# One perceiver block on one core: the state-space part spread over three batches, and the expansion to channels done by four 32-row products

## The chip, the cores and the metric

The kernel runs on one NeuronCore of a Trainium2 chip. The metric is the device time of one execution in microseconds; the time before is the median of three runs, 1502.03 us (1501.18 to 1503.05). All numbers below are microseconds unless they say otherwise.

## The reference, cut to what matters

128 sequences of 32 queries with 256 channels attend to 257 context rows each (16 heads of 16 channels), then pass a state-space layer and a mixture of experts:

```
x = x + cross_attention(layernorm(x), ctx, mask)      # (128, 32, 256), context (128, 257, 256)
x = x + state_space(layernorm(x))
x = x + experts(layernorm(x))                         # 8 experts, the best 2 of each token
```

Two details of it matter here. The softmax is divided out late: the kernel multiplies unnormalised probabilities with the values, and then multiplies each channel of the result with the reciprocal of its head's sum. And the state-space layer is `out = Y[0] / norm`:

```
proj = xs @ W_in.T                   # C, B and x of 256 columns each, and dt
conv_out = sum_k xp[:, k:k+s] * conv_w[:, k] + conv_b
A = A_param * softplus(dt + bias)
Y = ssd(xh, A, Bh, Ch)               # Y_diag = einsum(C, B, exp(segsum(A)), x)
norm = exp(cumA) * cumsum(exp(-cumA))
```

Only `Y[0]`, the result of the first sequence, is used, so `ssd` is computed once for 32 positions, and the norm for every sequence.

## The kernel before, in words

The first phase (`attend`, lines 115 to 1385) goes over 32 tiles of 128 tokens; a tile has four batches (sequences) b = 0 to 3 of 32 queries. The second (`experts`) goes over 71 tiles of tokens sorted by expert. The change is in the first alone.

Each engine has its own program, written out by hand as a function `tile(i)` with a loop over b; the engines meet in semaphores, and the order within an engine is the order of its `tile`. Tiles 0 to 3 and the last ones are unrolled, the rest is a hardware loop. The work is staggered: while TensorE weighs the values of batch n, it transposes the probabilities of n+1 and projects keys and values (k and v, 24 products in a split precision) of n+2. In each batch TensorE does `turn_c`, `project_k`, `project_v`, `turn_a`, `weigh_values`, `transpose_probs(.., 0)`, `turn_b`, `transpose_probs(.., 1)`, `scores`. `turn_a`, `turn_b` and `turn_c` hold the small products of the tiles before: expansion, attention's output, dt, the sums of the decay, the router.

PSUM has eight banks: K (keys, later the weighed values OT and the sums RP), V_ (values, and the second half of the transposed probabilities), four banks SC for the scores, PT, and M, which all the small products share one after the other. The names that the prediction follows:

- `px` (lines 1320 to 1330, GpSimd): per query the reciprocal of each head's sum, and the last context row's probability times it, laid out by group of heads, 128 queries and heads by 32 columns. `mm(RP, px, sel)` (line 492) is the last product of `weigh_values` and releases `o_ready`. ScalarE copies RP to `rp` (`take_rp`).
- `o_ready` also releases ScalarE's copy of the next values (`take_values`, line 724). The second `transpose_probs` writes the bank V_ and so waits for that copy (`v_done`, line 472).
- `expand` (line 512): four products with constant matrices `er` and `ep` bring the 32 rows of `rp` to 256 channels, twice (reciprocals and last probabilities), in M. VectorE's `weigh` (line 926) multiplies them with the weighed values and the last values; `attention_out` adds them.
- `ssd` (lines 572, 783 and 1136 for TensorE, ScalarE and VectorE): runs once, in batch 0 of tile 2, ahead of the second transposes. It projects the first sequence (24 instructions), VectorE convolves in a chain of linked instructions, TensorE forms C times B per head, then the segment sums, ScalarE takes the exponential, VectorE multiplies and masks 16 times into `w4` (each head's weights four times side by side), and 16 products with x fill all 128 rows of M, which ScalarE copies to `y0`. All of it is one chain over one bank; the other engines' tile work stands meanwhile.

Of the kernel before, what the change touches and what calls it, by code (L numbers as in the profile page):

```python
# [4 lines left out]
F32 = mybir.dt.float32  # L5
# [109 lines left out]
def attend(nc, xd, ctxd, ctxl, maskd, pard, wxbcd, cond, padd, wgd, wud, wdd, d_high, d_low, zbuf, table, outd, con, cst, wg, wu, wd,  # L115
# [7 lines left out]
    with own:  # L123
# [53 lines left out]
        px = sb("px", [P, 2, 2, NH, NG, 2])  # L177
# [42 lines left out]
        w4 = carve(H * P)[0:Q].rearrange("p (h b l) -> p h b l", h=H, b=TB)  # L220
# [4 lines left out]
        SC = [ps(f"sc{r}") for r in range(NG)]  # L225
# [3 lines left out]
        RP = K[0:2 * H, NH * 2 * Q:NH * 2 * Q + Q]  # L229
# [41 lines left out]
        NSOFT = len(ATANH) + 6  # L271
        PLAN = 10
# [30 lines left out]
        def _(sp):  # L303
# [77 lines left out]
            sp.wait_ge(ssd_act, 4)  # L381
# [28 lines left out]
        def _(pe):  # L410
# [161 lines left out]
            def ssd():  # L572

                pe.wait_ge(wxbc_in, 16)
                pe.wait_ge(a_done, 1)
                pe.wait_ge(norm_done, 1)
# [5 lines left out]
                pe.wait_ge(ssd_dve, 11)  # L582
# [4 lines left out]
                pe.wait_ge(ssd_act, 1)  # L587
                pe.wait_ge(ssd_dve, 12)
                mm(M[0:Q, :], cst("gt")[0:Q, :], at_[:, :, :].rearrange("p h l -> p (h l)")).then_inc(ssd_pe, 1)
                pe.wait_ge(ssd_act, 2)  # L590
# [4 lines left out]
                pe.wait_ge(ssd_dve, 14)  # L595
                for h in range(H):
                    last = mm(M[:, h * HD:(h + 1) * HD], w4[:, h, :, :].rearrange("p b l -> p (b l)"),
                              xs[:, h * HD:(h + 1) * HD])
                last.then_inc(ssd_pe, 1)
                pe.wait_ge(ssd_act, 4)  # L600


            def turn_a(i, b):
                if b == 0 and runs(i - 1):
                    if runs(i - 2):
                        pe.wait_ge(en_done, i - 1)
                    if isinstance(i, int) and i == 1:
                        pe.wait_ge(z1T_done, 3)
                    expand(i - 1)
# [13 lines left out]
            def turn_b(i, b):  # L623
                if b == 0 and (runs(i - 2) or runs(i - 3)):
                    if runs(i - 1):
                        pe.wait_ge(t_done, 2 * i)
                    sum_decay_and_rank(i - 2, i - 3)
                    if isinstance(i, int) and i == 2:
                        ssd()
# [15 lines left out]
            def turn_c(i, b):  # L645
                if b == 0 and runs(i - 1):
                    if runs(i - 2):
                        pe.wait_ge(norm_done, i - 1)
                    if runs(i - 3):
                        pe.wait_ge(chosen_done, i - 1)  # L650
                    project_out(i - 1)
# [4 lines left out]
                if b == 2 and runs(i - 2):  # L656
                    if runs(i - 1):
                        pe.wait_ge(dt_done, i)
                    turn_z3(i - 2)
                if b == 3 and runs(i - 1):  # L660
# [4 lines left out]
                    sum_a(i - 1)  # L665

# [19 lines left out]
            pe.wait_ge(blank_rows, 1)  # L686
# [25 lines left out]
        def _(act):  # L712
# [35 lines left out]
            def take_rp(i, b):  # L748
                n = 4 * i + b
                act.wait_ge(ou_done, n + 1)  # L750
                act.wait_ge(blank_rows, 1)
                if b == 0:
                    at_least(act, ex_ready, i)
                copy(rp[0:2 * H, b * Q:(b + 1) * Q], RP).then_inc(rp_done, 1)
# [28 lines left out]
            def ssd():  # L783
                act.wait_ge(ssd_pe, 2)
                copy(gs[:, :, :].rearrange("p h l -> p (h l)"), M[0:Q, :]).then_inc(ssd_act, 1)
                act.wait_ge(ssd_pe, 3)
                nc.scalar.activation(ls[:, :, :].rearrange("p h l -> p (h l)"), M[0:Q, :], ACT.Exp).then_inc(ssd_act, 1)
# [19 lines left out]
            def tile(i, k=None):  # L807
                for b in range(TB):
# [7 lines left out]
                    if b == 0 and runs(i - 2):  # L816
                        decays(i - 2)
                    if b == 2 and runs(i - 1):
# [7 lines left out]
                    if b == 0 and isinstance(i, int) and i == 2:  # L826
                        ssd()
# [8 lines left out]
                    if b == 3 and runs(i + 2):  # L836
                        take_z1T(i + 2)
                    if b != 0 and runs(i):
# [25 lines left out]
        def _(dve):  # L864
# [61 lines left out]
            def weigh(j):  # L926
# [3 lines left out]
                EX = M[:, :].rearrange("p (k a n) -> p k a n", k=2, a=NH)  # L930
# [205 lines left out]
            def ssd():  # L1136
                k = [0]

                def link(ins):
                    k[0] += 1  # L1140
                    ins.then_inc(ssd_dve, 1)
                    dve.wait_ge(ssd_dve, k[0])


                dve.wait_ge(ssd_pe, 1)
                link(V.memset(xp[:, :, 0:KC - 1], 0.0))
                link(V.tensor_copy(xp[:, :, KC - 1:], M[:, 0:NC * Q].rearrange("p (c l) -> p c l", c=NC)))
# [5 lines left out]
                link(V.tensor_tensor(cv[:, 0], xp[:, :, 0:Q], tap(0), ALU.mult))  # L1153
                for n in range(1, KC):
                    link(V.tensor_tensor(cv[:, 1], xp[:, :, n:n + Q], tap(n), ALU.mult))
                    link(V.tensor_tensor(cv[:, 0], cv[:, 0], cv[:, 1], ALU.add))
                link(V.tensor_tensor(cT, cv[:, 0], prm("convb").unsqueeze(2).broadcast_to([P, NC, Q]), ALU.add))
# [4 lines left out]
                link(last)  # L1162
                le = cst("le")[0:Q, :].unsqueeze(1).broadcast_to([Q, H, Q])
                link(V.tensor_tensor(at_, dtv[0:Q, 5, :].unsqueeze(2).broadcast_to([Q, H, Q]), le, ALU.mult))
                dve.wait_ge(ssd_act, 2)
                link(V.tensor_tensor(ws, gs, ls, ALU.mult))
                for h in range(H):
                    last = V.tensor_tensor(w4[:, h], ws[:, h, :].unsqueeze(1).broadcast_to([Q, TB, Q]),
                                           cst("le")[0:Q, :].unsqueeze(1).broadcast_to([Q, TB, Q]), ALU.mult)
                link(last)  # L1170
                assert k[0] == 14, k[0]
                dve.wait_ge(ssd_act, 4)

            def tile(i):
                for b in range(TB):
# [35 lines left out]
                    if b == 0 and runs(i + 2):  # L1211
                        statistics1(i + 2)
                    if b == 0 and runs(i - 1):
                        weigh(i - 1)
                        attention_out(i - 1)
                    if b == 1 and runs(i - 1):
# [27 lines left out]
                    if b == 0 and isinstance(i, int) and i == 2:  # L1244
                        ssd()
# [4 lines left out]
                    if b == 2 and runs(i - 1):  # L1250
                        soft_in(i - 1)

            V.memset(chosen[:, :], 0.0).then_inc(chosen_done, 1)
            V.memset(rp[:, :], 0.0).then_inc(blank_rows, 1)
# [3 lines left out]
            V.tensor_copy(tokf[:, :], cst("tok")).then_inc(init, 1)  # L1258
            dve.wait_ge(init, 2)
# [21 lines left out]
        def _(pool):  # L1281
# [38 lines left out]
            def last_probs(i, b):  # L1320
# [5 lines left out]
                for k in range(2):  # L1326
                    G.tensor_tensor(px[:, b % 2, k].rearrange("p a g h -> p g a h"),
# [53 lines left out]
            split_low(0, 2)  # L1381
            last_probs(0, 0)
# [384 lines left out]
```

## Time and profile before

| | |
|---|---|
| median of three runs | 1502.03 |
| the profiled execution | 1488.71 |
| its span | 1486.7 |
| TensorE busy | 1410.8 (95%) |
| VectorE busy | 1124.9 (76%) |
| ScalarE busy | 996.1 (67%) |
| GpSimd busy | 833.8 (56%) |
| share of TensorE in the chain that ended last | 84% |

The trace has each instruction's start and length. A matmul in fp32 runs as two instructions, and in a row of the timeline equal instructions that follow each other are merged (x8). Matmuls are pipelined: each takes some 0.2 to 0.4 from start to end, while the next starts 0.1 after it, so it is starts that tell what TensorE spends; the ends tell when others can go on. The busy share is an average over a loop in which TensorE is gapless, one tile with the state-space part, and the experts.

### The profile page before, as it was taken

What the parts mean: (1) busy time and instruction counts of PE and PEld (TensorE: products, weight loads), DVE (VectorE), ACT (ScalarE), POOL (GpSimd) and SP (SyncE); (2) the same over time, 40 slices, a digit from 0 to 9 for tenths busy, and PEclk for the clock granted to TensorE, in tenths of its full rate; (3) what the DMA queues carried; (4) which work ended last, traced back from release to release, by engine and by line L of the source; (5) the groups of instructions that cost most, each with busy time, mean ns of one, the idle gap of its engine ahead of it and who ended that gap; (6) DMA issues with size and microseconds to landing.
All of it is one profiled execution on the core that took longest, in us unless ns stands there. A gap on an engine that the chain in (4) does not pass through costs nothing.

```text
span 1486.7 us, 53570 instructions
## 1 busy us (share of the span) xinstructions
PE 1410.8 (95%) x15668; PEld 1288.0 (87%) x15669; DVE 1124.9 (76%) x3999; ACT 996.1 (67%) x2482; POOL 833.8 (56%) x1401
## 2 busy tenths in 40 slices
PE   6969999999999999999999998579999999999997
PEld 5858888888888888888888887379999999999997
DVE  3647888888888888888888886468878777787775
ACT  4726777777777777777777775067777776777674
POOL 3514665665666656656656553236666665565554
PEclk9969999999999999999999998589999999999999
DMA  6212464454433433433433321435655555555554
GB/s 189 67 30 73 120 200 136 144 192 131 122 98 96 127 93 99 122 101 90 126 96 106 86 70 55 159 120 149 162 141 151 158 142 145 144 163 142 141 147 111
DMA packets 102009, 183.80 MB, mean 124 GB/s; under 512 B 19393, under 2 KB 61377, under 8 KB 101793
## 3 DMA queue, kind: packets, MB, share of 16 engines
q1 hardware_dynamic: 86272, 164.35, 36.5%
q0 software_dynamic: 15680, 18.76, 7.1%
q8 instruction: 28, 0.46, 0.1%
q14 instruction: 29, 0.23, 0.1%
HBM read 152.63 MB, written 31.13 MB: 124 GB/s over the span
## 4 chain that ended last, share of the span: by engine, by line
PE 84%; DMA 2%; issue 2%; POOL 2%; DVE 1%; ACT 1%; POOLq 1%; DVEq 0%; ACTq 0%; SPq 0%
PE k L412 16%; PE m L412 12%; PE v_p L412 11%; PE y_p L1478 9%; PE up_p L1478 9%; PE gate_p L1478 8%; PE sc L412 5%; PE pt L476 5%; PE v_p L476 4%; PE ht_p L1517 3%; PE m L496 2%; DMA par<-zbuf,gi 2%; PE z_p L1484 1%; POOL gi L1668 1%; POOLq L1667 0%
## 5 line engine op out<-in xcount | busy, mean ns | idle before, releaser
L738 ACT ACTIVATE wd<-wd,nmx 128x257 f32<-128x257 f32 x512 | 255.7, 503 | 31.0 <-DVE nmx L884 26.7
L714 ACT ACTIVATE wd<-v_p 128x512 f32<-128x512 f32 x256 | 152.6, 596 | 163.8 <-PE k L412 136.5
L1305 POOL TENSOR_TENSOR ctx_lo<-wd,ctx_hi 128x516 fp32r<-128x516 f32 x128 | 167.0, 1304 | 130.5 <-ACT ctx_hi L714 130.5
L884 DVE CUSTOM_DVE_ANT_0 wd<-sc,wd 128x257 f32<-128x257 f32 x512 | 191.4, 421 | 63.6 <-PE sc L412 57.3
L1680 POOL DMA_INDIRECT out<-par,oi x71 | 113.5, 1599 | 146.5 <-ACT par L1586 145.9
L412 PE MATMUL k<-ctx_hi,wkh 128*128 128x256 f32 x512 | 159.3, 311 | 1.7 <-POOL ctx_lo L1305 1.4
L1557 ACT ACTIVATE uw_hi<-wu 128x1408 fp32r x71 | 98.3, 1385 | 85.1 <-PE up_p L1478 84.8
L1668 POOL COPY oi<-par 128x4 int32 x71 | 148.1, 2087 | 0.0
L1615 DVE TENSOR_TENSOR uw_lo<-wu,uw_hi 128x1408 fp32r<-128x1408 f32 x71 | 115.4, 1625 | 41.3 <-ACT uw_hi L1557 41.3
L412 PE MATMUL k<-ctx_lo,wkh 128*128 128x256 f32 x512 | 145.3, 284 | 0.0
L1615 DVE TENSOR_TENSOR gw_lo<-wg,gw_hi 128x1408 fp32r<-128x1408 f32 x71 | 115.4, 1625 | 39.2 <-ACT gw_hi L1557 39.2
L412 PE MATMUL k<-ctx_hi,wkl 128*128 128x256 f32 x512 | 145.0, 283 | 0.0
L412 PE MATMUL v_p<-wvh,ctx_lo 128*128 128x256 f32 x512 | 143.7, 281 | 0.0
L412 PE MATMUL v_p<-wvh,ctx_hi 128*128 128x256 f32 x512 | 143.4, 280 | 0.0
L412 PE MATMUL v_p<-wvl,ctx_hi 128*128 128x256 f32 x512 | 142.6, 279 | 0.0
L873 DVE TENSOR_SCALAR kT<-k,par 128x256 f32<-128x256 f32 x256 | 114.1, 477 | 24.3 <-PE k L412 23.6
L1668 POOL COPY gi<-par 128x4 int32 x71 | 122.2, 1721 | 10.3 <-issue 5.7
L1478 PE MATMUL y_p<-wd,hT_hi 128*128 x426 | 121.1, 284 | 1.9 <-DVE hT_lo L1615 1.9
L1478 PE MATMUL y_p<-wd,hT_lo 128*128 x426 | 120.5, 283 | 0.0
L1478 PE MATMUL y_p<-dl,hT_hi 128*128 128x256 f32 x426 | 120.1, 282 | 0.0
L1557 ACT ACTIVATE gw_hi<-wg 128x1408 fp32r x71 | 98.1, 1382 | 13.9 <-PEq L123 8.7
L1674 POOL DMA_INDIRECT par<-zbuf,gi x71 | 73.2, 1031 | 60.3 <-POOL gi L1668 53.3
(200 smaller groups left out, 4678.8 us busy)
## 6 DMA issues: line engine op xcount, KB each, us to landing
dl<-d_low SPq DMA_DIRECT2D x71, 768.0 KB, 4.4
wd<-in_ctx SPq DMA_DIRECT2D x128, 258.0 KB, 2.7
wd<-in_mask SPq DMA_DIRECT2D x512, 32.1 KB, 1.8
wd<-in_wd SPq DMA_DIRECT2D x24, 256.0 KB
d_high<-wd SPq DMA_DIRECT2D x24, 256.0 KB
d_low<-wd SPq DMA_DIRECT2D x24, 256.0 KB
wd<-d_high SPq DMA_DIRECT2D x8, 768.0 KB, 9.2
wg<-in_wg SPq DMA_DIRECT2D x8, 704.0 KB
```

The lines of the kernel that those rows point to most:

```text
L412: return nc.tensor.matmul(out, lhsT, rhs, start=start, stop=stop)
L476: last = nc.tensor.transpose((PT, V_)[d][:, o:o + P], pr[:, g, t * P:(t + 1) * P], ident)
L714: return nc.scalar.activation(out, in_, ACT.Copy, **kw)
L738: nc.scalar.activation(pr[:, g, :], sm[:, g, :], ACT.Exp, bias=nmx[:, g:g + 1], scale=-1.0, accum_out=rsum[:, g:g + 1]).then_inc(exp_done, 1)
L873: V.tensor_scalar(kT[:, b % 2, a, 0:LAST], K2[:, a, :], prm("bk")[:, a:a + 1], None, ALU.add).then_inc(k_done, 1)
L884: V.tensor_tensor_reduce(sm[:, g, :], SC[g][:, 0:S], msk[:, b, :], -1.0, 3.0e38, ALU.add, ALU.min, nmx[:, g:g + 1]).then_inc(max_done, 1)
L1305: G.tensor_tensor(ctx_lo[:, b % 2], ctx[:, b], ctx_hi[:, b % 2].bitcast(F32), ALU.subtract).then_inc(lo_done, 1)
L1478: return nc.tensor.matmul(out, lhsT, rhs, start=start, stop=stop)
L1557: nc.scalar.activation(dst, src, ACT.Copy).then_inc(done, 1)
L1615: V.tensor_tensor(dst, src, hi.bitcast(F32), ALU.subtract).then_inc(done, 1)
L1668: G.tensor_copy(dst.unsqueeze(1), tab[:, bass.ds(col, 1), :]).then_inc(done, 1)
L1680: G.indirect_dma_start(outd[:, :], bass.IndirectOffsetOnAxis(oi[:, s, 1:2].bitcast(U32), 0), yb[:, s, :], None, compute_op=ALU.add).then_i ...
```

## The change

- `expand` uses one constant `spread` (128x128) and four row groups: rows 32r to 32r+31 of `rp` against the same rows of `spread`, each into its own score bank. For that the four kinds of sums must stand on different row groups: `px` gets 128 columns, 32 per kind with 8 in use (the rest set to zero once), RP and `rp` have all 128 rows.
- As the expansion now writes score banks, it waits for the maxima of the batch before them, and the scores of batch 2 wait for `weigh`. It no longer waits for M's users (`en_done`), and the sums in `turn_b` no longer wait for `weigh`.
- VectorE does `weigh` and `attention_out` before the statistics of a later tile.
- `ssd` is cut into pieces: the projection ahead of batch 3 of tile 1, the convolution on VectorE at that batch's end, the segment sums ahead of batch 0 of tile 2 in the bank PT, the rest (`ssd_mix`) where all of it was. The mask is multiplied in once, on C times B; the 16 masked copies fall away, and the last products are 64 of 32x32 instead of 16 of 32x128.

```
 def expand(j):
     pe.wait_ge(rp_done, 4 * (j + 1))
-    for k, e in enumerate(("er", "ep")):
-        for a in range(NH):
-            o = (k * NH + a) * P
-            last = mm(M[:, o:o + P], cst(e)[:, a * P:(a + 1) * P], rp[:, :])
+    if runs(j + 1):
+        pe.wait_ge(max_done, 4 * (4 * (j + 1) + 2))
+    for r in range(NG):
+        rows = slice(r * Q, (r + 1) * Q)
+        last = mm(SC[r][:, 0:P], spread[rows, :], rp[rows, :])
     last.then_inc(ex_ready, 1)
...
-        px = sb("px", [P, 2, 2, NH, NG, 2])
+        px = sb("px", [P, 2, 2 * NH, Q])
+        spread = sb("spread", [P, P])
...
-        RP = K[0:2 * H, NH * 2 * Q:NH * 2 * Q + Q]
+        RP = K[:, NH * 2 * Q:NH * 2 * Q + Q]
...
-    mm(RP, px[:, b % 2].rearrange("p k a g h -> p (k a g h)"), cst("sel")).then_inc(o_ready, 1)
+    mm(RP, px[:, b % 2].rearrange("p k n -> p (k n)"), cst("sel")).then_inc(o_ready, 1)
...
 def scores(i, b):
+    if b == 2 and runs(i - 1):
+        pe.wait_ge(t_done, 2 * i)
...
+def ssd_project():
+    pe.wait_ge(wxbc_in, 16)
+    pe.wait_ge(dt_done, 1)
...
+def ssd_sums(n):
+    pe.wait_ge(pt_done, 2 * n - 1)
+    pe.wait_ge(ssd_dve, SSD_A)
+    mm(PT[0:Q, :], cst("gt")[0:Q, :], at_[:, :, :].rearrange("p h l -> p (h l)")).then_inc(ssd_pe, 1)
+
+def ssd_mix():
+    pe.wait_ge(norm_done, 1)
+    pe.wait_ge(ssd_dve, SSD_C)
...
+    pe.wait_ge(ssd_act, 2)
+    pe.wait_ge(ssd_dve, SSD_C + 2)
+    for h in range(H):
+        for b in range(TB):
+            last = mm(M[b * Q:(b + 1) * Q, h * HD:(h + 1) * HD], ws[:, h, :], xs[:, h * HD:(h + 1) * HD])
...
 # VectorE
-    for h in range(H):
-        last = V.tensor_tensor(w4[:, h], ws[:, h, :].unsqueeze(1).broadcast_to([Q, TB, Q]),
-                               cst("le")[0:Q, :].unsqueeze(1).broadcast_to([Q, TB, Q]), ALU.mult)
+    ssd_step(V.tensor_tensor(gs, M[0:Q, :].rearrange("p (h l) -> p h l", h=H), le, ALU.mult))
+    ssd_step(V.tensor_tensor(ws, gs, ls, ALU.mult))
...
 # TensorE: where the pieces go
+    if b == 2 and isinstance(i, int) and i == 1:      # turn_c
+        ssd_project()
...
-        pe.wait_ge(dt_done, i)                        # turn_b, b == 3: turn_z1 in tile 1
+        pe.wait_ge(ssd_dve, SSD_X)
...
     sum_a(i - 1)                                      # turn_c, b == 3
+    if isinstance(i, int) and i == 1:
+        ssd_sums(TB * (i + 1) + 1)
```

## Rows read from the trace of the kernel before

**Rows 1.** Busy time by stage: us, busy (xcount) of each engine, clock, DMA, GB/s.
```profile
138.08:904.99 766.91, 765.53 (x10528) 673.50 (x10527) 630.28 (x3079) 556.28 (x1733) 465.04 (x973) 1.00 0.40 116
81.33:138.08 56.75, 45.31 (x439) 37.39 (x437) 29.53 (x126) 20.92 (x65) 13.47 (x32) 0.73 0.15 38
86.00:116.70 30.70, 20.14 (x88) 14.91 (x88) 11.05 (x40) 6.18 (x17) 1.29 (x1) 0.50 0.02 4
```

**Rows 2.** Timeline of TensorE, steady tile: start, length, engine, line, operation, count.
```profile
247.64 0.28 PE L412 MATMUL v_p<-wvh,ctx_lo 128*128 128x256 f32 x1
247.75 1.05 PE L412 MATMUL m<-rp,con 128*128 128x128 f32 x8
248.74 0.65 PE L412 MATMUL k<-wd 128*32 128x64 f32 x32
249.21 0.23 PE L412 MATMUL k<-con,px 128*32 128x32 f32 x2
249.36 0.66 PE L476 MATMUL pt<-con,wd 128*128 128x128 f32 x4
...
250.22 0.37 PE L412 MATMUL m<-chosen,con 128*128 128x8 f32 x2
250.44 0.63 PE L476 MATMUL v_p<-con,wd 128*128 128x128 f32 x4
251.01 0.69 PE L412 MATMUL sc<-kT,qbd 32*64 32x257 f32 x16
251.63 1.13 PE L412 MATMUL m<-par,aT 128*128 128x256 f32 x4
```

**Rows 3.** Timeline of TensorE, tile 1 (values product to weighing).
```profile
61.98 0.28 PE L412 MATMUL v_p<-wvh,ctx_lo 128*128 128x256 f32 x1
62.19 0.65 PE L412 MATMUL k<-wd 128*32 128x64 f32 x32
```

**Rows 4.** Timeline of TensorE, steady tile, behind the scores.
```profile
271.94 0.40 PE L412 MATMUL m<-dtv,con 128*128 128x16 f32 x2
```

**Rows 5.** Timeline of TensorE, third and fourth batch of the steady tile.
```profile
264.48 0.63 PE L476 MATMUL v_p<-con,wd 128*128 128x128 f32 x4
...
269.70 0.22 PE L412 MATMUL k<-con,px 128*32 128x32 f32 x2
...
270.35 0.38 PE L496 MATMUL m<-con,wd 128*128 128x128 f32 x2
270.77 0.63 PE L476 MATMUL v_p<-con,wd 128*128 128x128 f32 x4
```

**Rows 6.** Timeline of ScalarE, the same two batches.
```profile
263.80 0.60 ACT L714 ACTIVATE wd<-v_p 128x512 f32<-128x512 f32 x1 [1.20 <-PE k L412]
...
270.03 0.60 ACT L714 ACTIVATE wd<-v_p 128x512 f32<-128x512 f32 x1 [1.16 <-PE k L412]
```

**Rows 7.** Timeline of TensorE in the state-space part.
```profile
84.57 3.98 PE L412 MATMUL m<-z2T,wg 128*128 128x32 f32 x24 [0.84 <-DVE dtv L1012]
93.09 1.92 PE L412 MATMUL m<-wg 128*32 128x256 f32 x4 [4.54 <-DVE wg L1160]
95.68 1.91 PE L412 MATMUL m<-wg,con 32*32 32x512 f32 x2 [0.68 <-ACT wg L714]
...
102.49 6.97 PE L412 MATMUL m<-wg 32*128 32x16 f32 x32 [3.61 <-DVE wg L1168]
110.52 1.08 PE L476 MATMUL v_p<-con,wd 128*128 128x128 f32 x4 [1.05 <-ACT wd L714]
```

**Rows 8.** Timeline of VectorE ahead of and in the state-space part.
```profile
77.23 0.16 DVE L1007 TENSOR_TENSOR dtv<-sc,par 128x16 f32<-128x16 f32 x1
...
88.73 0.36 DVE L1147 COPY wg<-m 128x192 f32<-128x192 f32 x1
...
98.32 0.68 DVE L1166 TENSOR_TENSOR wg<-wg 32x512 f32<-32x512 f32 x1 [4.57 <-ACT wg L787]
```

**Rows 9.** Chain of waits, the end of attention: start, length, what.
```profile
926.86 2.09 PE m L412 x8
```

More of the change, by code:

```diff
@@ L224, in attend @@
         K2 = K[:, 0:NH * LAST].rearrange("p (a t) -> p a t", a=NH)
-        SC = [ps(f"sc{r}") for r in range(NG)]
+        SCORES = own.enter_context(nc.psum_tensor("sc", [P, NG, 512], F32))
+        SC = [SCORES[:, r, :] for r in range(NG)]
         PT = ps("pt")
@@ L271, in attend @@
         NSOFT = len(ATANH) + 6
+        SSD_X, SSD_A, SSD_C = 2, 3, 12
         PLAN = 10
@@ L593, in ssd @@
                 last.then_inc(ssd_pe, 1)
-                pe.wait_ge(ssd_act, 3)
-                pe.wait_ge(ssd_dve, 14)
-                for h in range(H):
[L597 to L600, printed above, removed]
+                pe.wait_ge(ssd_act, 2)
[3 more added lines that the diff above has]
+                        last = mm(M[b * Q:(b + 1) * Q, h * HD:(h + 1) * HD], ws[:, h, :], xs[:, h * HD:(h + 1) * HD])
+                last.then_inc(ssd_pe, 1)
+                pe.wait_ge(ssd_act, 3)
             def turn_a(i, b):
                 if b == 0 and runs(i - 1):
[L605 to L608, printed above, removed]
                     expand(i - 1)
@@ L624, in turn_b @@
                 if b == 0 and (runs(i - 2) or runs(i - 3)):
-                    if runs(i - 1):
-                        pe.wait_ge(t_done, 2 * i)
                     sum_decay_and_rank(i - 2, i - 3)
                     if isinstance(i, int) and i == 2:
-                        ssd()
+                        ssd_mix()
                 if b == 1 and runs(i - 2):
@@ L665, in turn_c @@
                     sum_a(i - 1)
+                    if isinstance(i, int) and i == 1:
+                        ssd_sums(TB * (i + 1) + 1)
             def tile(i):
@@ L750, in take_rp @@
                 act.wait_ge(ou_done, n + 1)
-                act.wait_ge(blank_rows, 1)
                 if b == 0:
                     at_least(act, ex_ready, i)
-                copy(rp[0:2 * H, b * Q:(b + 1) * Q], RP).then_inc(rp_done, 1)
+                copy(rp[:, b * Q:(b + 1) * Q], RP).then_inc(rp_done, 1)
             def take2(dst, ready, done, j):
@@ L781, in gate_exp, with ssd_exp, ssd_out @@
                 nc.scalar.activation(sv[:, 1, 0:1], sv[:, 0, 0:1], ACT.Exp).then_inc(gate_e, 1)
-            def ssd():
+            def ssd_exp():
                 act.wait_ge(ssd_pe, 2)
-                copy(gs[:, :, :].rearrange("p h l -> p (h l)"), M[0:Q, :]).then_inc(ssd_act, 1)
-                act.wait_ge(ssd_pe, 3)
-                nc.scalar.activation(ls[:, :, :].rearrange("p h l -> p (h l)"), M[0:Q, :], ACT.Exp).then_inc(ssd_act, 1)
+                nc.scalar.activation(ls[:, :, :].rearrange("p h l -> p (h l)"), PT[0:Q, :], ACT.Exp).then_inc(ssd_act, 1)
+            def ssd_out():
                 act.wait_ge(ssd_pe, 4)
@@ L817, in tile @@
                         decays(i - 2)
+                    if b == 0 and isinstance(i, int) and i == 2:
+                        ssd_exp()
                     if b == 2 and runs(i - 1):
@@ L837, in tile @@
                         take_z1T(i + 2)
+                    if b == 0 and isinstance(i, int) and i == 2:
+                        ssd_out()
                     if b != 0 and runs(i):
@@ L1134, in plan_tiles, with ssd_step, ssd_conv @@
                               ).then_inc(info_done, 1)
[L1136 to L1142, printed above, removed]
-                dve.wait_ge(ssd_pe, 1)
-                link(V.memset(xp[:, :, 0:KC - 1], 0.0))
-                link(V.tensor_copy(xp[:, :, KC - 1:], M[:, 0:NC * Q].rearrange("p (c l) -> p c l", c=NC)))
+            ssd_steps = [0]
+            def ssd_step(ins):
+                ssd_steps[0] += 1
+                ins.then_inc(ssd_dve, 1)
+                dve.wait_ge(ssd_dve, ssd_steps[0])
+            def ssd_conv():
+                le = cst("le")[0:Q, :].unsqueeze(1).broadcast_to([Q, H, Q])
+                dve.wait_ge(ssd_pe, 1)
+                ssd_step(V.memset(xp[:, :, 0:KC - 1], 0.0))
+                ssd_step(V.tensor_copy(xp[:, :, KC - 1:], M[:, 0:NC * Q].rearrange("p (c l) -> p c l", c=NC)))
+                assert ssd_steps[0] == SSD_X
+                dve.wait_ge(a_done, 1)
+                ssd_step(V.tensor_tensor(at_, dtv[0:Q, 5, :].unsqueeze(2).broadcast_to([Q, H, Q]), le, ALU.mult))
+                assert ssd_steps[0] == SSD_A
                 taps = prm("convw").rearrange("p (c k) -> p c k", k=KC)
@@ L1161, in ssd, with ssd_weights @@
                                            cst("bm8").unsqueeze(2).broadcast_to([P, n8, Q]), ALU.mult)
-                link(last)
+                ssd_step(last)
+                assert ssd_steps[0] == SSD_C
+            def ssd_weights():
                 le = cst("le")[0:Q, :].unsqueeze(1).broadcast_to([Q, H, Q])
[L1164 to L1167, printed above, removed]
-                    last = V.tensor_tensor(w4[:, h], ws[:, h, :].unsqueeze(1).broadcast_to([Q, TB, Q]),
-                                           cst("le")[0:Q, :].unsqueeze(1).broadcast_to([Q, TB, Q]), ALU.mult)
-                link(last)
-                assert k[0] == 14, k[0]
-                dve.wait_ge(ssd_act, 4)
+                dve.wait_ge(ssd_pe, 3)
+                ssd_step(V.tensor_tensor(gs, M[0:Q, :].rearrange("p (h l) -> p h l", h=H), le, ALU.mult))
+                dve.wait_ge(ssd_act, 1)
+                ssd_step(V.tensor_tensor(ws, gs, ls, ALU.mult))
+                dve.wait_ge(ssd_act, 3)
             def tile(i):
@@ L1215, in tile @@
                         attention_out(i - 1)
+                    if b == 0 and runs(i + 2):
+                        statistics1(i + 2)
                     if b == 1 and runs(i - 1):
@@ L1251, in tile @@
                         soft_in(i - 1)
+                    if b == 3 and isinstance(i, int) and i == 1:
+                        ssd_conv()
             V.memset(chosen[:, :], 0.0).then_inc(chosen_done, 1)
-            V.memset(rp[:, :], 0.0).then_inc(blank_rows, 1)
+            V.memset(px[:, :, :, :].rearrange("p b k n -> p (b k n)"), 0.0).then_inc(blank_rows, 1)
             V.memset(pay[:, :, :].rearrange("p k c -> p (k c)"), 0).then_inc(init, 1)
@@ L1258, in _ @@
             V.tensor_copy(tokf[:, :], cst("tok")).then_inc(init, 1)
+            V.tensor_copy(spread[:, :].rearrange("p (h d) -> p h d", d=HD),
+                          cst("sel")[:, 0:P // HD].unsqueeze(2).broadcast_to([P, P // HD, HD])).then_inc(blank_rows, 1)
             dve.wait_ge(init, 2)
```

34 lines of the change are left out of this document (12 added, 22 removed).

## The prediction

> **What bounds the kernel now.** I read the stages first, then the order of time on TensorE, then the other engines at the places that looked tight. In the attention loop 28 tiles take 766.91 us, 27.39 each, and TensorE is busy for 765.53 of them at the full clock [rows 1]: every ns that TensorE issues more or less per tile counts. The one tile in which the state-space part (SSD) runs takes 56.75, so 29.36 more, much of it at a granted clock of 0.50 [rows 1]. The expert phase is not touched. The change acts on three things: the expansion (once a tile), the product with px (once a batch, four a tile), and the SSD part (once).
>
> **The expansion.** Today four products, two instructions each, take from 247.75 to 248.74; from the last values product to the next stage it is 1.10 (247.64 to 248.74) [rows 2]. Where no expansion stands between, the same step takes 0.21 (61.98 to 62.19) [rows 3]. So it costs 0.89. One 128-column instruction takes (1.05 - 0.28)/7 = 0.11. The 0.21 is such a stream plus 0.10, which every change of the array's shape shows. The new form has four products on 32 rows each, in four banks. The nearest row is the scores: 32x64 pieces, eight side by side, two rounds of 257 columns, 0.62 from 251.01 to 251.63 [rows 2]. Two streams of 257 columns are 0.43, so 0.19 is first load, issue and changeover. With 128 columns the streams are 0.22; the load is twice as wide (+0.05) and there are fewer pieces (-0.02): 0.44. The values product now also hands over to another shape (0.21 for 0.11): 0.65 instead of 1.10, **-0.45 a tile**. Bounds: if the wide loads of the row groups came one after another, eight times 0.11 plus a last stream and changeover, 1.28, **+0.18**; if nothing but the two streams counted, -0.6.
>
> **The product with px.** It keeps its 32 columns of result but its weights grow from 32 to 128 columns, so it leaves the 32-column shape of the products before it, and has the full shape. Today the pair starts at 249.21 and the transposes at 249.36: 0.15, of which 0.10 is the changeover, so about 0.04 for the pair [rows 2]. The same kind of pair with full weights and few columns, chosen, takes 0.22 (250.22 to 250.44) although it streams 8 columns: its loads set the pace, 0.11 each [rows 2]. So TensorE pays 0.22 - 0.04 = +0.18 a batch (bounds: 0.02, if the loads hid behind the products before; 0.23, if the transposes' first load were pushed out too).
> What waits for the pair is worse off. The pair dtv, the first behind a changeover, takes 0.40 from start to end [rows 4]; px today 0.22 to 0.23. With the changeover now ahead of it (it starts 0.11 later), its end comes **0.29 later**. ScalarE's copy of the values waits for that, and the second transposes wait for the copy. In the third batch the copy ends at 263.80 + 0.60 = 264.40 and the transposes start at 264.48; in the fourth 270.63 and 270.77, while TensorE's own work ran out at about 270.57 (270.35 and two instructions of 0.11) [rows 5, 6]. These two batches have no slack and pay 0.29 each. The first two have longer products ahead of those transposes (in the first dtv, lg and chosen [rows 2]) and pay 0.18. Per tile 2 x 0.18 + 2 x 0.29 = **+0.94**. That ScalarE now copies 128 rows of RP in place of 32 costs nothing, as its time goes by columns (rp copies are off the path).
> One rule of the Trainium skill bears on this. The rows show 0.11 for a full-width load, 0.03 from one px instruction to the other. The page "TensorE: Matmul & The Clock Gate", section "LDWEIGHTS (loading the stationary operand)", says that a load's time goes by its columns, at columns/1.2 ns, however many rows it has: an estimate by it is 107 for 27 ns, +0.16 a batch, 20 us over 128 batches, and with it alone the sum below would end 8 us lower, as it has no waiting copy in it.
>
> **Waits that move.** The wait for weigh's two products goes from ahead of the decay sums to ahead of the scores; no row of the steady tile shows an idle time there [rows 2]. The expansion now waits for the four maxima of the next batch, which VectorE has behind it by its own order, and VectorE does weigh before the statistics. All at nothing, hidden under TensorE's 24 k and v products. Without that cover each would cost an instruction or two of VectorE's, 0.36 to 0.68 [rows 8], a tile.
> Per tile: -0.45 + 0.94 = **+0.49**; 28 tiles: +13.7. Tiles 1, 2 and 31 have stalls that take part of it: +1.0 together. Steady sum **+14.7**.
>
> **The SSD part.** Before, in its tile [rows 7, 8]: a wait of 0.84 and the projection (84.57, 24 instructions at half clock), VectorE's convolution from 88.73 (TensorE idle 4.54), products at 93.09, sums at 95.68, transposes, the masking of 16 weights (TensorE idle 3.61), 32 instructions from 102.49, copies, until 110.52; then 6.2 us at half clock until 116.70. New:
> - projection in the tile before: 24 loads of 0.11 = 2.7 on TensorE's path, at full clock;
> - z1's transposes wait until VectorE has copied the projection. VectorE gets there behind the second head and a (77.23 + 0.16), then needs 0.45 for memset and copy and semaphore time: 1.3 that TensorE waits;
> - the sums as a product of their own: 1.91 at half clock [rows 7], so 1.0;
> - the convolution (the 4.54 for which TensorE idles today [rows 7], less the 0.6 that come before the sums: 3.9) delays VectorE's maxima and keys; the 24 k and v products, 0.12 each, hide 2.9 of it, the rest comes back before the expansion and weigh: 0.8;
> - the wait for norms, with VectorE late: 1.7 in place of 0.84;
> - the mix: four products 0.9, masking at the 0.68 of the same shape [rows 8] and handover 0.9, the second multiply or transposes and copy of x 1.0, 128 small instructions at the k<-wd pace (0.47 for 32 [rows 2]) 1.9, handover and copy of y 0.5: 5.2. Of the 16 maskings nothing is left.
> Sum 12.7. TensorE streams little in these stretches, and today the clock falls after just such a stretch and costs 3.1 behind it. I take 3.9 for that: 16.6 against 29.36, **-12.7**. Bounds: full clock throughout -16.9; clock down already from the projection on, the work between doubled, -8.
> In the tail, at half clock, the last expansion (2.09 [rows 9]) is on the chain: -1.2, px there +0.5: **-0.7**.
>
> **Sum**: 14.7 - 12.7 - 0.7 = +1.3. The profiled execution took 1488.71 (span 1486.7), which becomes 1490.0; the runs' median is 1502.03, of which none of these stages is known to hold the other 13, so I carry the difference over: **1503.3**.
>
> **Rivals.**
> - Clock falls early. For it: the clock is 0.50 from 86.00 on, though TensorE was busy there, with loads more than streams; the projection now brings 2.7 us of that a tile earlier. Against: it is followed by dense k and v products. Saves 8 only: 1508.
> - Full clock throughout: the waits are now short and split. Against: the mix still has 5 us of handovers. Saves 16.9: 1499.
> - Wide px loads are hidden (0.02 a batch): then a tile changes by -0.37, so 11 less instead of 15 more, with the rest 1478; with part of it hidden, around 1490. For it: 32-column loads hide today. Against: the chosen and dtv pairs don't.
> - The row groups' loads come one after another: it decides once the eight loads cost 0.3 more than the streams hide (9 us in 30 tiles); in full +0.18 in place of -0.45, 30 tiles, +19: 1522, slower. Against: the scores' sixteen loads fit into 0.62.
> - The change doesn't do what it says on the maskings or products: excluded by the diff, no time of its own.
>
> **Chances.** Forecast (gain and loss cancel) 0.43; clock early 0.17; full clock 0.15; px loads hidden in whole or part 0.16; loads serial 0.09. Range of the forecast itself 1498 to 1508; with the clock's cases and partly hidden px loads 1489 to 1513, which leaves out the ends of the last two. About 0.2% (3 us) is what a measurement of this kernel can tell from no change. Faster: 0.15 of the px case, 0.09 of full clock, 0.09 of the forecast's own spread = 0.33. Slower: 0.09 serial, 0.14 clock early, 0.12 of the forecast = 0.35. Same: 0.32.
>
> **What would show it.** The distance between two expansions in the loop: 27.88 for 27.39. From the values product to weigh's products: 0.65. From the px pair's first to the transposes: 0.22 or more, and the second transposes of the last two batches 0.29 later than now. The tile with the SSD mix near 39, the one before it 5 to 6 longer than it was. It is wrong if the tile distance falls (px loads hidden), or exceeds 28.2 (loads serial), or if SSD's two tiles together give back less than 8 or more than 17.

## The result, and the profile after

| | before | changed |
|---|---|---|
| median of 7 and 7 runs on one chip | 1502.72 (1501.18 to 1503.64) | 1506.13 (1505.37 to 1509.19) |
| ratio, 95% interval | | 1.0028 [1.0016, 1.004] |
| the profiled execution (span) | 1488.71 (1486.7) | 1506.13 (1504.1) |
| attention loop, 28 tiles [rows 1] | 766.91 | 798.01 |
| the tile with the SSD mix [rows 1] | 56.75 | 39.20 |
| TensorE at half clock, one stretch [rows 1] | 30.70 | 13.65 |
| TensorE busy | 1410.8 | 1415.3 |

The kernel became 3.4 us slower, and 1506.13 lies within the forecast's range (1503.3, 1489 to 1513). The profiled execution of before, 1488.71, lies outside that chip's own timed runs of the same kernel (1501.18 to 1503.64), so the two profiles can't be subtracted as a whole. Below they are compared tile by tile.

By stage, the windows of the changed kernel: the loop, the SSD tile, the half-clock stretch (columns as in [rows 1]).
```profile
129.67:927.68 798.01, 776.94 (x10528) 673.90 (x10527) 629.69 (x3078) 559.52 (x1731) 465.73 (x973) 1.00 0.39 111
90.47:129.67 39.20, 34.86 (x506) 28.29 (x506) 23.54 (x102) 21.62 (x70) 13.58 (x33) 0.83 0.22 57
93.88:107.53 13.65, 10.79 (x170) 7.38 (x171) 5.01 (x18) 4.04 (x13) 1.27 (x1) 0.50 0.08 22
```
The loop is 31.1 us longer (28.50 a tile against 27.39), while TensorE's busy time in it grew by 11.4 only, from 765.53 to 776.94. So a good part of the loss is TensorE standing still, where before [rows 1] it was gapless. The SSD tile is 17.6 shorter.

TensorE in the steady tile, from the expansion on; it answers to [rows 2].
```profile
271.61 0.50 PE L414 MATMUL sc<-rp,spread 32*128 32x128 f32 x8
272.04 0.65 PE L414 MATMUL k<-wd 128*32 128x64 f32 x32
272.63 0.41 PE L414 MATMUL k<-con,px 128*128 128x32 f32 x2
272.87 0.63 PE L480 MATMUL pt<-con,wd 128*128 128x128 f32 x4
...
274.49 0.69 PE L414 MATMUL sc<-kT,qbd 32*64 32x257 f32 x16
275.86 1.10 PE L414 MATMUL m<-par,aT 128*128 128x256 f32 x4 [0.68 <-DVE dtv L1022]
```
From the expansion to weigh's products it is now 0.43, where it was 0.99; px starts 0.24 ahead of the transposes instead of 0.15. Those are the forecast's terms. Then comes what it does not have: from the scores to attention's output 1.37 instead of 0.62, with 0.68 of idling behind the norms (line 1022). The list of waits gives it for the whole kernel:
```profile
PE m L414 <- DVE dtv L1022: 18.2, 25, 2.1
```
Its longest, 2.1, is in the SSD part; the other 24 are the loop's, 16 us together. In the same list of before the norms stand with 1.5 in 2 waits, none of them the loop's.

VectorE in before, where the statistics (line 911, as 913 behind it) are done while the expansion runs, and the norms' multiply is line 1012:
```profile
248.25 0.43 DVE L911 BATCH_NORM_STATS2 st<-wd 128x6 f32<-128x256 f32 x1
...
248.87 0.42 DVE L931 TENSOR_TENSOR t<-m,ou 128x256 f32<-128x256 f32 x1
...
250.71 0.16 DVE L1012 TENSOR_TENSOR dtv<-m,dtv 128x16 f32<-128x16 f32 x1
```
VectorE in the tile of the changed kernel shows what the wait is made of.
```profile
269.50 0.43 DVE L894 CUSTOM_DVE_ANT_0 wd<-sc,wd 128x257 f32<-128x257 f32 x1 [1.54 <-PE sc L414]
...
272.57 0.42 DVE L941 TENSOR_TENSOR t<-sc,ou 128x256 f32<-128x256 f32 x1
272.91 0.41 DVE L942 TENSOR_TENSOR t<-sc,vl 128x256 f32<-128x256 f32 x1
273.36 0.80 DVE L952 SCALAR_TENSOR_TENSOR aT<-t,par 128x128 f32<-128x128 f32 x2
274.08 0.41 DVE L921 BATCH_NORM_STATS2 st<-wd 128x6 f32<-128x256 f32 x1
274.59 0.18 DVE L923 BATCH_NORM_AGGREGATE mv<-st 128x2 f32<-128x6 f32 x1
...
275.21 0.16 DVE L1022 TENSOR_TENSOR dtv<-m,dtv 128x16 f32<-128x16 f32 x1
```
The maxima at 269.50 begin after 1.54 of idling for the scores of the fourth batch; then come the other maxima and the keys, one wait of 0.70 for ScalarE, and work without a pause up to the norms at 275.21, the statistics (274.08, 274.59) among it. The scores that it waited for, on TensorE, and GpSimd at that time:
```profile
267.72 0.69 PE L414 MATMUL sc<-kT,qbd 32*64 32x257 f32 x16
```
```profile
267.88 0.96 POOL L1358 DMA_INDIRECT slot_table<-pay,ri  x1 [0.30 <-issue]
```
The scores' last product ends at 267.72 + 0.69 = 268.41. VectorE begins 1.09 later. The release comes late in this way in all 28 tiles of the loop in this trace, by 0.9 against the traces below, each time with GpSimd's second indirect DMA (0.96 long) in progress when the scores end. In the trace of before [rows 1] no release of the scores is late, nor is one in its second trace, below, though that DMA is in progress there too at the end of the fourth batch's scores.

TensorE in the SSD part; it answers to [rows 7].
```profile
74.59 2.87 PE L414 MATMUL m<-z2T,wg 128*128 128x32 f32 x24
...
82.91 0.44 PE L500 MATMUL m<-con,wd 128*128 128x128 f32 x2 [1.14 <-DVE wg L1159]
...
84.66 1.04 PE L414 MATMUL pt<-wg,con 32*32 32x512 f32 x2
...
90.47 0.50 PE L414 MATMUL sc<-rp,spread 32*128 32x128 f32 x8 [1.70 <-DVE nmx L894]
91.26 0.65 PE L414 MATMUL k<-wd 128*32 128x64 f32 x32 [0.29 <-DVE kT L883]
...
95.00 1.91 PE L414 MATMUL m<-wg 128*32 128x256 f32 x4 [2.14 <-DVE dtv L1022]
97.68 0.61 PE L601 MATMUL m<-con,wg 128*32 128x128 f32 x2 [0.77 <-DVE wg L1184]
...
101.17 1.11 PE L480 MATMUL v_p<-con,wd 128*128 128x128 f32 x4 [0.50 <-ACT y L723]
```

### The profile page after: what moved, and what is told of

It reads as the page before. It is cut to its first block and busy times, and to the rows that moved or that the text cites. A ratio compares the mean times of both kernels' runs of the same rounds, so it can differ in the third digit from the quotient of the medians.

```text
span 1504.1 us, 53622 instructions
## 1 busy us (share of the span) xinstructions
PE 1415.3 (94%) x15764; PEld 1280.6 (85%) x15765; DVE 1124.3 (75%) x3985; ACT 999.4 (66%) x2481; POOL 834.5 (55%) x1401
## 5 line engine op out<-in xcount | busy, mean ns | idle before, releaser
L1342 POOL TENSOR_TENSOR rr<-wd,rr 128x4 f32<-128x4 f32 x128 | 25.5, 199 | 186.6 <-DVE rr L901 180.6
```

## The experiments

Before ran on three more chips, at 1486.35 (9 runs), 1483.95 (15) and 1484.17 (17), 16 to 19 us faster than on the chip of the first comparison. Ratios below are against before on the same chip. "A tile" is the median distance between two expansions in the loop; before's is 27.38 in both of its traces.

**SSD alone.** The changed kernel with `expand`, px, RP, the order of `weigh` and its waits as before.
```
-                for r in range(NG):
-                    rows = slice(r * Q, (r + 1) * Q)
-                    last = mm(SC[r][:, 0:P], spread[rows, :], rp[rows, :])
+                for k, e in enumerate(("er", "ep")):
+                    for a in range(NH):
+                        ...
+                        last = mm(M[:, o:o + P], cst(e)[:, a * P:(a + 1) * P], rp[:, :])
```


> The kernel before with the state-space part alone spread as in the change (expansion, px and VectorE's order as before). Theory (gain of the state-space part is real, what ate it is in the loop): the two tiles together 10 to 11 us shorter than before (tile 1 near 33.5, tile 2 near 39), the loop unchanged at 27.39 in the profile, so 1492 against 1502.7. Rival (the spreading itself brought little, the change's loop is innocent): within 3 us of before.

Measured: 1473.83, ratio 0.9918 [0.9905, 0.9932], so -12.5. Windows of the loop and of the tile with the mix:
```profile
126.01:893.79 767.78, 766.16 (x10528) 673.69 (x10527) 630.60 (x3078) 555.83 (x1731) 465.49 (x973) 1.00 0.40 116
89.55:126.01 36.46, 32.81 (x507) 27.29 (x508) 23.68 (x105) 21.98 (x70) 13.51 (x32) 0.91 0.24 61
```
The loop is that of before (767.78 against 766.91). The gain lies in tiles 1 and 2, which take 33.89 + 36.46 = 70.35 for 26.74 + 56.75 = 83.49: -13.1. The forecast had -12.7; the 10 to 11 expected of this run was too little; it is what these tiles give in the changed kernel (10.6).

**Wide px alone.** Before, with px and RP of 128 columns and rows, the 32 rows that count first, the expansion as it was.
```
-        px = sb("px", [P, 2, 2, NH, NG, 2])
+        px = sb("px", [P, 2, P])
-        RP = K[0:2 * H, NH * 2 * Q:NH * 2 * Q + Q]
+        RP = K[:, NH * 2 * Q:NH * 2 * Q + Q]
```


> The kernel before with px, RP and rp made 128 wide and nothing else; the expansion is the old one. Theory (two exposed full-width loads behind a changeover, and a release 0.29 later in the last two batches): tile 27.39 + 0.94 = 28.33, 28 us slower, 1530. Rival (the width costs TensorE nothing, the loss of the changed kernel is all waits for VectorE): tile 27.4, same time.

Measured: 1512.26, ratio 1.0175 [1.0161, 1.0189], +25.9. Its loop:
```profile
139.43:932.41 792.98, 788.48 (x10528) 690.31 (x10527) 636.07 (x3079) 556.88 (x1733) 464.75 (x973) 1.00 0.38 112
```
28.31 a tile, +0.93, where the forecast's term is +0.94. The first two batches take 0.18 and 0.19 more, the last two 0.28 and 0.29.

**The changed kernel with px as four column products.** Four pairs, each with 32 columns of px, each into its own 32 rows of RP.
```
-                mm(RP, px[:, b % 2].rearrange("p k n -> p (k n)"), cst("sel")).then_inc(o_ready, 1)
+                for r in range(NG):
+                    last = mm(RP[r * Q:(r + 1) * Q], px[:, b % 2, r, :], cst("sel"))
+                last.then_inc(o_ready, 1)
```


> The changed kernel with the px product as four products of 32 columns, each into its own column group, so that the shape stays that of the products before it. Theory: px costs about 0.06 to 0.1 a batch in place of 0.22, the last two batches win 0.25 or more each; in the first batch the win is swallowed by the wait for the norms, which grows by as much. Tile 28.57 - 0.75 = 27.8, 20 us faster than the changed kernel, 1486. Rival (px is hidden, the norm wait sets the tile): no more than 3 us.

Measured: 1475.47, ratio 0.992 [0.9906, 0.9934], so -10.9. TensorE around px:
```profile
266.84 0.65 PE L414 MATMUL k<-wd 128*32 128x64 f32 x32
267.31 0.24 PE L414 MATMUL k<-con,px 128*32 128x32 f32 x8
267.48 0.66 PE L480 MATMUL pt<-con,wd 128*128 128x128 f32 x4
```
The pair becomes eight instructions, and still px starts 0.17 ahead of the transposes (0.15 in before, 0.24 in the changed kernel). The px product keeps the 128x32 shape of its neighbours, so no changeover is ahead of it. Against the changed kernel's 784.2 on the other chips (below) the loop gives 16.9 back:
```profile
129.15:896.47 767.32, 757.04 (x11200) 660.41 (x11199) 629.66 (x3078) 552.60 (x1731) 464.10 (x974) 1.00 0.40 116
```
That is 27.41 a tile, 0.60 less than the changed kernel's 28.01; 0.75 was expected, counted from the trace with the late releases. The busy time is 757.04, so 10.3 are still idle. Attention's output again waits 0.30 in each tile:
```profile
270.12 1.10 PE L414 MATMUL m<-par,aT 128*128 128x256 f32 x4 [0.30 <-issue]
```
As TensorE comes to it still earlier, the norms' wait has grown: from the scores to attention's output it is 0.99, 0.37 more than in before, where the changed kernel has 0.18 more.

**Slot writes a batch earlier.** The changed kernel with the indirect DMAs of `write_slots` in batch 2 instead of 3.
```
-                    if b == 3 and runs(i - 3):
+                    if b == 2 and runs(i - 3):
                         write_slots(i - 3)
```


> The changed kernel with GpSimd's two slot writes (indirect DMAs) of a tile issued at the end of batch 2 instead of batch 3. In the changed kernel the release of the scores issued in batch 3 reaches VectorE 0.95 late in 27 tiles, while the second slot write runs, and project_out then waits 0.75 for the norms. Theory A (the slot write holds that release up): the delay leaves this place, tile near 27.85, 19 us faster, 1487. Theory B (VectorE's new order and TensorE's earlier arrival make the wait, the late release is an accident of the record): tile stays within 0.1 of 28.57 and the time within 3 us.

Measured: 1492.69, ratio 1.0042 [1.0029, 1.0056], 28.01 a tile against 28.58 in the first trace of the changed kernel. It looks like a gain of 0.57 a tile, but the chip was another. So the changed kernel itself had to be measured away from the first chip.

**The changed kernel again**, not altered.

> The changed kernel itself, so that it stands beside the others on one chip. The chip of the experiments runs the kernel before in 1486, the chip of the first comparison in 1503. Theory A (the late release of the scores in 27 tiles is a trait of that other chip and stretched the kernel before there too): here no late release, tile 28.05, 8 us slower than before. Theory B (the late release belongs to the change): tile 28.57, 22 us slower.

Measured: 1493.09, ratio 1.0058 [1.0045, 1.0072], 28.01 a tile, the loop 784.42. No release is late in this trace. The slot writes had gained nothing.

**The third chip: before again, the changed kernel a third time, the slot writes again.**

> The kernel before once more, for its own profile on the chip of the experiments. Theory (the chips differ by 16 us outside the attention loop's instructions or by late releases): on a chip near 1485 the tile is 27.39 and no release is late; on a chip near 1503 either the tile is longer, with scores released late, or the experts take longer.

> The changed kernel once more. On a chip near 1485: tile 28.01, 9 slower than before. On a chip near 1503: late releases as in its first profile, tile 28.57, 3 to 4 slower than before.

> The slot writes in batch 2 once more. On the first chip of the experiments it was level with the changed kernel on the second (tile 28.01 both), so where no release is late the place of the slot writes is worth nothing. On a chip near 1503, theory A (the slot writes hold the release up): faster than after_third by up to 15, theory B: the same.

Measured: before 1484.43, ratio 0.9996 [0.9982, 1.001]; changed 1492.87, 1.006 [1.004, 1.0079]; slot writes earlier 1493.17, 1.006 [1.0041, 1.008]. Loops of before and of the changed kernel there:
```profile
137.79:904.66 766.87, 765.53 (x10528) 673.53 (x10527) 630.41 (x3079) 556.26 (x1733) 465.18 (x973) 1.00 0.39 116
```
```profile
130.65:914.89 784.24, 776.90 (x10527) 673.87 (x10526) 628.95 (x3078) 555.21 (x1731) 464.62 (x974) 1.00 0.38 113
```
784.24 - 766.87 = 17.4, or 0.62 a tile. Here the scores of the fourth batch end at 266.87 + 0.69 = 267.56, and VectorE begins 0.20 later instead of 1.09:
```profile
266.87 0.69 PE L414 MATMUL sc<-kT,qbd 32*64 32x257 f32 x16
```
```profile
267.76 0.43 DVE L894 CUSTOM_DVE_ANT_0 wd<-sc,wd 128x257 f32<-128x257 f32 x1 [0.65 <-PE sc L414]
```
GpSimd's indirect DMA is in progress here as well when these scores end:
```profile
267.04 0.96 POOL L1358 DMA_INDIRECT slot_table<-pay,ri  x1 [0.31 <-issue]
```
This is so in 28 tiles of this trace, of after_again's and of both of before's, and none of these releases is late. So the DMA's being there does not delay the release by itself; what differs in the first trace is not shown.

Behind the expansion, VectorE's first product of `weigh` and its multiply of the norms:
```profile
271.33 0.42 DVE L941 TENSOR_TENSOR t<-sc,ou 128x256 f32<-128x256 f32 x1 [0.42 <-PE sc L414]
...
273.79 0.16 DVE L1022 TENSOR_TENSOR dtv<-m,dtv 128x16 f32<-128x16 f32 x1
```
Attention's output starts at 274.44, 3.68 behind the expansion:
```profile
270.76 0.50 PE L414 MATMUL sc<-rp,spread 32*128 32x128 f32 x8
...
274.44 1.10 PE L414 MATMUL m<-par,aT 128*128 128x256 f32 x4
```
It still waits: from the scores to it are 0.79, against 0.62 in before. The loop's norm waits have left the list of waits, in which only the 2.1 of the SSD part stands:
```profile
PE m L414 <- DVE dtv L1022: 2.1, 1, 2.1
```
So the place of the slot writes is without effect where no release is late. Whether it would change the late releases on the first chip was not shown, since no experiment ran there.

**Statistics later.** VectorE's statistics of a later tile (0.6 in all, lines 921 and 923) behind the norms instead of ahead of them.
```
                     if b == 0 and runs(i - 1):
                         weigh(i - 1)
                         attention_out(i - 1)
-                    if b == 0 and runs(i + 2):
-                        statistics1(i + 2)
...
                     if b == 0 and runs(i - 2):
                         scale_y(i - 2)
+                    if b == 0 and runs(i + 2):
+                        statistics1(i + 2)
```


> The changed kernel with VectorE's statistics of a later tile moved to the end of batch 0, behind the norms. Theory (project_out waits for the norms, because VectorE has weigh, attention_out and the statistics between the reciprocals and the norms while TensorE now comes 0.28 earlier): the wait of 0.18 a tile goes, tile 27.88, 5 us faster than the changed kernel. Rival (the wait hangs on o_ready and the heads, not on VectorE's order): tile unchanged within 0.03.

Measured: 1486.11, ratio 1.0014 [1.0005, 1.0023], 7.0 less than the changed kernel on the same chip (1493.09), and still 2.2 more than before. A tile is 27.87, the number that the forecast had for it (27.88), and from the scores to attention's output it is 0.62 again:
```profile
127.77:908.22 780.45, 776.03 (x10527) 674.19 (x10526) 633.86 (x3078) 554.91 (x1731) 464.38 (x974) 1.00 0.39 114
```
The loop gives 4.0 of the 7.0. Most of the rest lies ahead of tile 2, where the two traces differ by 2.3 (91.52 and 89.21 at its expansion), and this is not shown to be the edit's: there two traces of one program, after_third and slots_b2_again (whose edit acts from tile 3 on), differ by 2.5 on one chip.

**Both: four column products and statistics later.**

The two edits above together.

> Both mends: px as four products of 32 columns in their own column groups, and the statistics behind the norms. px_cols alone had a tile of 27.41 with 0.37 of it a wait for the norms. Theory: that wait goes, tile 27.04, 10 us faster than px_cols and 21 faster than before, 1465. Rival (another release is next, such as the copy of the values in the last two batches or weigh ahead of the scores): tile 27.3 or more, at most 4 us faster than px_cols.

Measured: 1463.56, ratio 0.9859 [0.9844, 0.9874], 20.4 faster than before and the best of all; a tile is 27.05.
```profile
128.36:886.09 757.73, 755.42 (x11200) 660.05 (x11199) 630.21 (x3078) 552.58 (x1731) 464.51 (x974) 1.00 0.40 117
```
TensorE is busy 755.42 of 757.73, all but gapless again.

**The expansion alone**, with four column products and late statistics, the SSD part as in before. Of the SSD's edits it has none, such as:
```
-    if b == 2 and isinstance(i, int) and i == 1:
-        ssd_project()
...
+    for h in range(H):
+        last = V.tensor_tensor(w4[:, h], ws[:, h, :].unsqueeze(1).broadcast_to([Q, TB, Q]),
```

> The kernel before with the expansion of the change and both mends (px as four products of 32 columns, the statistics behind the norms), the state-space part as it was. Theory (the two parts of the change add up, each acts on its own stretch): tile 27.05, 9 to 10 us faster than before, 1474 on a chip where before takes 1484; together with the 12.5 of the state-space part this gives the 20 to 22 of cols_stats_late. Rival (the parts share a gain): more than 13 or less than 6.

Measured: 1475.79, ratio 0.9935 [0.9919, 0.9952], -8.4; a tile is 27.07.
```profile
136.30:894.31 758.01, 755.85 (x11200) 660.45 (x11199) 628.45 (x3078) 553.04 (x1731) 465.46 (x974) 1.00 0.40 117
```
With SSD alone (-12.5) that makes -20.9, and both together measured -20.4: in the medians the two halves add up within their intervals (some 2 us each). The traces do not show it stage by stage: tiles 1 and 2 fall from 81.68 here to 73.48 in cols_stats_late, by 8.2, where SSD alone had 13.1, and 3.7 of the rest stand in the stretch behind the last expansion, mostly the experts, on which no edit acts.

## Why the prediction was right, and where it was right by luck

**The loop's terms** held to a few hundredths. From the last values product to weigh's it is 0.64 (0.21 + 0.43) for 1.10, the -0.45 of the expansion; the serial-loads rival (+0.18) and "two streams only" are out. px costs +0.93 a tile: 0.18 and 0.19 on TensorE in the first two batches, 0.28 and 0.29 in the last two, where the values' copy releases the transposes. The fourth batch of the changed kernel, TensorE and then ScalarE; it answers to [rows 5, 6]:
```profile
265.91 0.41 PE L414 MATMUL k<-con,px 128*128 128x32 f32 x2
266.16 0.64 PE L480 MATMUL pt<-con,wd 128*128 128x128 f32 x4
266.63 0.38 PE L500 MATMUL m<-con,wd 128*128 128x128 f32 x2
267.16 0.63 PE L480 MATMUL v_p<-con,wd 128*128 128x128 f32 x4
```
```profile
266.42 0.60 ACT L723 ACTIVATE wd<-v_p 128x512 f32<-128x512 f32 x1 [1.46 <-PE k L414]
```
The copy ends at 266.42 + 0.60 = 267.02, the transposes start at 267.16, and TensorE's own work ran out at 266.63 + 0.22 = 266.85, as the forecast's chain has it. The rivals with hidden px loads are out. Column products show what hidden costs: 0.02 in each of the first two batches. The Trainium skill's page "TensorE: Matmul & The Clock Gate", "Part 3: Packing small matmuls — row/col tiling", says that products in different column groups run concurrently in the array; the trace agrees with it: from the first of the four column products to the transposes (eight instructions) it is 0.17, where one 32-column pair had 0.15 and the wide pair 0.24.

**The step that failed** is "Waits that move", all of which the forecast put "at nothing". It looked for idle time in the rows of before and found none at attention's output, but did not work out how much slack was there. The change uses it up from both sides. TensorE comes to attention's output sooner: 3.88 behind the expansion in before (247.75 to 251.63), 3.50 without a wait, as stats_late shows: 0.38 sooner. VectorE could come sooner too, since `weigh` is released sooner, but the statistics eat that up: before, VectorE did them while the expansion ran and had the norms' multiply at 250.71, 2.96 behind the expansion; now it idles 0.42 for the expansion (up to 271.33), does the statistics behind `weigh` and `attention_out`, and has the multiply 273.79 - 270.76 = 3.03 behind it. With the statistics later it is 2.50. The rows of before give the slack: where attention's output waits, it starts 0.65 behind the multiply (273.79 to 274.44), and in before it starts 0.92 behind it (250.71 to 251.63), so 0.27 of slack. TensorE's 0.38 and VectorE's 0.07 are 0.45, and 0.45 - 0.27 = 0.18 is the wait that was measured (0.79 for 0.62). The order costs 28.01 - 27.87 = 0.14 a tile (0.03 of the wait is made up before the next batch), 4 us in the loop. The forecast's bound for this step, "an instruction or two of VectorE's, 0.36 to 0.68", was too high for the chips without late releases and its value too low.

On the first chip the same wait is 0.75 instead of 0.18, since VectorE starts late: the scores' semaphore reaches it 0.9 later in 28 tiles. In the loop that is 798.01 - 784.24 = 13.8. What delays it, and whether before has it there too, stays open (the indirect DMA alone does not, as the third chip shows): the first chip's timed runs of before are 16 to 19 us above those on the others, and the profile of before (1488.71) is not from such a run. That both kernels lose there fits the ratio of 1.0028, which is smaller than the 1.006 of the other chips; it was not shown.

**The SSD part**, -12.7 forecast and -12.5 measured alone. Piece by piece, forecast and the rows of the changed kernel, from start to start: projection 2.7 and 2.7; wait for z1 1.3 and 1.14; sums 1.0 and 0.97; convolution 0.8 and 1.70 + 0.29, as VectorE's maxima and keys do not catch up under the 24 products; wait for the norms 1.7 and 2.14; the mix 5.2 and 101.17 - 95.00 = 6.17, all at half clock. That is 15.1, and the half clock behind it, 6.4 long, costs up to 3.2: 18.3 for a forecast of 16.6. (In the forecast's own working 3.9 - 2.9 leaves 1.0, not 0.8, for the convolution, and 29.36 - 12.7 is 16.7, not 16.9; neither changes the outcome.) In the whole changed kernel the two tiles gave 83.49 - 72.93 = 10.6 back (9.6 on the third chip), in SSD alone 13.1. About 1.0 of the difference is the loop's +0.49 a tile, which the forecast counts elsewhere. Two more things differ. The half clock holds for 13.7 us or 17.1 in the changed kernel, for 10.2 in SSD alone; and the expansion now waits for the maxima (1.70 at 90.47), where SSD alone has a wait of 1.35 for ScalarE (line 781). In the first trace the clock falls once, at 93.88, while TensorE waits for the norms. In the other two traces of the changed kernel it falls twice, and the first time is right behind the projection, for 3.41; this is the window in the trace of the third chip, in which the projection ends at 77.45:
```profile
77.67:81.08 3.41, 3.41 (x18) 3.41 (x18) 1.06 (x5) 0.00 (x0) 0.00 (x0) 0.50 0.64 182
```
Tile 1 takes 34.8 there for 33.7 in the first trace. So "full clock" is out, and "clock falls early" came true in part, in some executions: 1.1, where that rival had 4.7 (8 saved instead of 12.7).

**The tail** is -0.7 in the trace of the third chip (20.91 to 20.24 between the last two expansions), as forecast; the last expansion takes 0.81 where it took 2.09 [rows 9]:
```profile
947.92 0.81 PE L414 MATMUL sc<-rp,spread 32*128 32x128 f32 x8
```

**Forgotten**: tile 0. The first expansion comes 2.4 later (54.28 to 56.71 on the third chip). Four wide px are 1.0 to 1.5 of it, as px_wide and slots_b2_again (55.30 on the same chip) show. The rest is the clock at the start: in the trace of the changed kernel the record of the granted clock begins, at full, at 19.64, and until then the products take about twice as long (eight of them 2.07 for 1.16); in before it begins at 13.87. It is not the change's: in slots_b2_again, the same program in tile 0, it begins at 13.29 and the eight take 1.16. Why executions differ in this stays open.

**The sum.** On the third chip, from the traces: loop +17.4, tiles 1 and 2 -9.6, start +2.4, tail -0.7: +9.5, and the medians say +8.7. The two profiled executions as a whole differ by 5.4 (1483.8 and 1489.2), because the stretch behind the last expansion, mostly the experts, is 4.1 shorter in the trace of the changed kernel (554.1 for 558.2). It varies from 554 to 560 over the traces. Part of that is the half clock at the end of attention, which ends 50.5 behind the last expansion there and 54.3 in before; the rest was not taken apart, so the sum of the stages is good to a few us only. The forecast had +1.3. It is 7 to 8 short, of which the norms' wait is 4, tiles 0 to 2 the rest. On the chip of the first comparison the difference was only 3.4, and there the forecast looks better than its reasoning was. As a difference its range, -13 to +11, held both cases; its chance for "slower by over 0.2%" was 0.35, and that is what happened everywhere.

## What to carry to other kernels

Where no idle time shows at a wait, work out its slack: what one engine gains and the other loses from the change add up against it, and here 0.38 and 0.07 met a slack of 0.27. A product that widens its weights from 32 to 128 columns costs its load, its changeover, and what waits behind its end; write it as four column products instead, if the results go to separate rows. And profile both kernels on the same chip, twice: a difference of 0.57 a tile between two traces was not that of the edit, since the unaltered kernel had it too.

## What the runs showed that was not expected

- Chips differ more than this change is worth: before took 1502.72 on one and 1484 to 1486 on three others.
- On the first of them, in the changed kernel, the scores' semaphore reached VectorE some 0.9 us later than elsewhere in 28 tiles, during an indirect DMA of GpSimd (0.96). The traces of that kernel from two other chips have the same DMA at the same place and no late release.
- The granted clock ahead of the loop differs between executions of one program: a short half clock of 3.41 us right behind the projection in two of three traces of the changed kernel, and, at the start, products at the pace of the half clock until 19.6 in one trace and not in another.
- Two instructions of VectorE (line 952) took 0.80 in the first trace, where two of GpSimd's (lines 1332 and 1336) ran beside them, and 0.61 in the third, where these were all but done when they began.
